# Ten first maxima of the next batch row computed beside steps 20 to 29 of the second attention, and the first maximum row turned before the overlapped stretch

## The reference

```python
# first attention: 16 heads of 8, two softmaxes of half heads, differential
a1 = softmax(q1 @ k1.T * scale); a2 = softmax(q2 @ k2.T * scale)
x = layernorm(x + rms_normed((a1 - lam * a2) @ v) @ wo)
# first network: weights and activations rounded to FP4 by blocks of 16
x = layernorm(x + fp4_linear(silu(fp4_linear(x, w_gate)) * fp4_linear(x, w_up), w_down))
# second attention: 16 query heads over 4 key heads of 64, rotary, causal
x = layernorm(x + softmax(causal(q @ k.T * scale)) @ v @ Wo + bo)
# second network: one of 8 experts for each token, relu, times the router's probability
x = layernorm(x + expert[argmax(x @ Wr)](x) * gate)
```

## Time and profile before

| | us |
|---|---|
| timed runs: lowest, median, highest | 1240.26, 1248.33, 1250.12 |
| profiled execution, its time | 1242.78 |
| profiled execution, span of its instructions | 1241.0 |
| `attention1(0)`, first to last score product (L1660) | 311.9 to 402.4 |
| `attention1(1)`, the same | 593.0 to 688.5 |
| first to last exponential of `overlap(1)` | 441.5 to 574.9 |
| first to last exponential of `overlap(2)` | 729.7 to 862.5 |

### The profile page before, as it was taken

How to read it: one execution, slowest core, us unless ns; L and a number is a source line. 1 busy time by engine, 2 the same in 40 slices (tenths; PEclk the granted TensorE clock), 3 DMA queues, 4 the chain that set the end, 5 groups by cost and what they waited for, 6 DMA issues and landing times.

```text
span 1241.0 us, 19493 instructions
## 1 busy us (share of the span) xinstructions
PE 1011.3 (81%) x6865; PEld 507.5 (41%) x6865; DVE 783.2 (63%) x1765; ACT 619.4 (50%) x1554; POOL 444.8 (36%) x545
## 2 busy tenths in 40 slices
PE   1888747889998788999988888999988829989754
PEld 1222321233454332555444442455444528344554
DVE  4898449882776688751787678770787451666421
ACT  1287514775367245774376334677177405157213
POOL 3000110301787214001776414000776450677411
PEclk7598855899999875899998875899999959999957
DMA  6300031121022001321013000320000014100051
GB/s 147 95 2 3 24 96 35 36 49 31 1 63 50 1 2 31 114 79 41 0 44 77 1 2 10 128 87 16 18 1 10 1 35 185 32 1 10 1 202 57
DMA packets 54096, 56.41 MB, mean 45 GB/s; under 512 B 13736, under 2 KB 45808, under 8 KB 53232
## 3 DMA queue, kind: packets, MB, share of 16 engines
q1 hardware_dynamic: 51968, 51.50, 14.1%
q0 software_dynamic: 1024, 2.10, 0.6%
q10 hardware_dynamic: 1008, 1.57, 0.5%
HBM read 42.77 MB, written 16.20 MB: 48 GB/s over the span
## 4 chain that ended last, share of the span: by engine, by line
PE 50%; DVE 21%; ACT 10%; issue 8%; POOL 5%; DMA 4%; SPq 1%; ACTq 0%; POOLq 0%; DVEq 0%
PE ps L1618 9%; DVE mx L987 8%; PE ps L1601 5%; PE ps L1647 5%; PE ps L1687 4%; PE ps L1660 4%; PE ps L1677 3%; ACT PROB L1317 3%; PE ps L1425 3%; PE ps L1419 2%; PE ps L1521 2%; PE ps L1436 2%; PE ps L1562 2%; DVE mx L1117 2%; ACT PROB L1275 2%
## 5 line engine op out<-in xcount | busy, mean ns | idle before, releaser
L987 DVE TENSOR_REDUCE mx<-ps 128x1 f32<-128x512 f32 x512 | 323.3, 684 | 82.1 <-PE ps L1562 79.9
L1275 ACT ACTIVATE PROB<-ps 128x512 f32<-128x512 f32 x512 | 276.8, 601 | 148.8 <-PE ps L1601 147.5
L576 POOL TENSOR_SCALAR PROB<-PROB,rsum 128x128 f32<-128x128 f32 (+3 forms) x224 | 229.6, 1036 | 76.6 <-DVE rsum L1122 76.2
L1317 ACT ACTIVATE PROB<-ps,mx 128x128 f32<-128x128 f32 (+3 forms) x256 | 133.1, 526 | 170.2 <-DVE mx L1117 169.9
L1562 PE MATMUL ps<-kst,qst 24*128 24x512 bf16 x512 | 156.4, 470 | 43.0 <-DVE mx L987 21.3
L1618 PE MATMUL ps<-PROB,v 128*32 128x256 f32 x2048 | 181.2, 446 | 3.1 <-ACT OREG L1284 2.7
L1601 PE MATMUL ps<-qst,kst 27*128 27x512 bf16 x512 | 139.8, 445 | 25.6 <-ACT PROB L1275 13.2
L1117 DVE TENSOR_REDUCE mx<-ps 128x1 f32<-128x128 f32 (+3 forms) x256 | 113.0, 484 | 69.2 <-PE ps L1662 68.9
L557 POOL CAST mparts<-mx 128x16 bf16<-128x16 f32 x32 | 7.0, 218 | 393.3 <-DVE mx L987 371.0
L1677 PE MATMUL ps<-cst,PROB 128*128 128x128 f32 x640 | 110.4, 292 | 41.9 <-ACT PROB L1332 18.2
L1660 PE MATMUL ps<-MREG,QREG 64*128 64x384 f32 (+3 forms) x512 | 108.4, 501 | 0.0
(11 more groups left out here) (220 smaller groups left out, 1361.8 us busy)
## 6 DMA issues: line engine op xcount, KB each, us to landing
wexp<-expert_rows SPq DMA_DIRECT2D x44, 514.0 KB, 5.2
qk_terms<-RREG SPq DMA_DIRECT2D x42, 128.0 KB, 2.1
qst<-qk_terms SPq DMA_DIRECT2D x16, 192.0 KB
RREG<-sorted_x SPq DMA_DIRECT2D x4, 704.0 KB, 4.7
sorted_y<-RREG SPq DMA_DIRECT2D x4, 704.0 KB, 3.9
kst<-qk_terms SPq DMA_DIRECT2D x12, 192.0 KB
expert_rows<-in_L_ffn_W_dram SPq DMA_DIRECT2D x8, 256.0 KB
expert_rows<-in_L_ffn_W_dram SPq DMA_DIRECT2D x4, 512.0 KB
```

The source lines that it names most:

```text
L576: pool.tensor_scalar(tile, tile, rsum1[:, 2 * v + half:2 * v + half + 1], None, ALU.mult).then_inc(scaled1, 1)
L987: dve.tensor_reduce(mx0[:, ga % 2, col:col + 1], ps[:, max_bank(k, MAX_SLOT[n]), :], AX, ALU.max, negate=True).then_inc(slot0_free, 1)
L1275: act.activation(prob0[:, s % 2, q % 4, q % 8 // 4], ps[:, s0_banks[q % len(s0_banks)], :], ACT.Exp, scale=float(HD0) ** -0.5).then_inc(ex ...
L1317: act.activation(prob1[:, half, at:at + w], ps[:, a1_bank(v, half), 0:w], ACT.Exp, bias=mx1[:, col:col + 1], accum_out=sum1[:, col:col + 1 ...
```

## The change

Ten maxima (n = 0 to 9) of row nx move to steps 20 to 29 of the second attention, one at the end of each step, in bank 7. The lead of steps 32 to 35 then holds the next 18 maxima (n = 10 to 27) and the first turned row, so that 28 maxima and one row precede the stretch; POOL's splitting of group 0 moves to step 33, and in the stretch the steps up to (0, 0) hold none of them. The wait for the terms stays with n = 0 and so moves to step 20; a wait for the sum of the first attention (`att0_sum`, the last reader of bank 7) joins it, and the wait for all exponentials moves to n = 10. Step 31's use of bank 7 waits until the tenth maximum is read. It concerns rows 2 and 3: `attention1(0)`, `overlap(1)`, `attention1(1)` and `overlap(2)`.

```diff
-LEAD = 18
+SINGLE, LEAD = 10, 29
+LEAD_END = (0, 0)
...
-LEAD_V = {32: ((-4, 3), (-3, 0), (-3, 1)), 33: ((-3, 2), (-3, 3)), 34: ((-2, 0), (-2, 1)), 35: ((-2, 2), (-2, 3))}
+SINGLE_V = {20 + _n: _n for _n in range(SINGLE)}
+LEAD_V = {32: ((-2, 0), (-2, 1), (-2, 2)), 33: ((-2, 3), (-1, 0)), 34: ((-1, 1), (-1, 2)), 35: ((-1, 3), (0, 0))}
...
 def max_bank(k, at):
 
+    if k >= 2 and at < SINGLE:
+        return 7
     if k >= 2 and at < LEAD:
         return 2 + at % 2
...
                 for g in range(NG):
-                    if k < BATCH:
+                    if k < BATCH and (g or k < 2):
                         max_parts0(k, g)
...
                     turn(r + 1, r + 2, v, rounds)
+                    if v == 33 and r + 2 < BATCH:
+                        max_parts0(r + 2, 0)
...
+            def maximum0(n, k):
...
+                dve.wait_ge(slot0_full, SLOTS * k + MAX_SLOT[n] + 1)
...
+                dve.tensor_reduce(mx0[:, ga % 2, col:col + 1], ps[:, max_bank(k, MAX_SLOT[n]), :], AX, ALU.max,
+                                  negate=True).then_inc(slot0_free, 1)
...
-                    if k < BATCH:
+                    if k < BATCH and (k < 2 or (s, c) > LEAD_END):
                         maxima0(s, c, k)
...
                     if nx < BATCH:
+                        if v in SINGLE_V:
+                            maximum0(SINGLE_V[v], nx)
                         for s, c in LEAD_V.get(v, ()):
                             maxima0(s, c, nx)
...
+            def score0(n, k):
...
+                if n == 0:
+                    pe.wait_ge(terms_in, 16 * 2 * HF * (k + 1))
+                    if k >= 2:
+                        pe.wait_ge(att0_sum, k)
+                if n == SINGLE and k >= 2:
+                    pe.wait_ge(exp1_done, 2 * NV * (k - 1))
+                if max_before(k, at) is not None:
+                    pe.wait_ge(slot0_free, SLOTS * k + max_before(k, at) + 1)
+                pe.matmul(ps[:, max_bank(k, at), :], qst[rows, n // 16, P * qt:P * (qt + 1)], kst[rows, n // 16, :],
+                          start=True, stop=True).then_inc(slot0_full, 1)
...
-                        scores0(s, c, k)
+                        if k < 2 or (s, c) > LEAD_END:
+                            scores0(s, c, k)
...
                         pe.wait_ge(xq_ready, k + 1)
                         pe.wait_ge(att0_sum, k + 1)
+                        if 2 <= nx < BATCH:
+                            pe.wait_ge(slot0_free, SLOTS * nx + SINGLE)
                         transpose_tiles(xq, 7, x_turned)
...
                     turn(v)
                     if nx < BATCH:
+                        if v in SINGLE_V:
+                            score0(SINGLE_V[v], nx)
                         for s, c in LEAD_V.get(v, ()):
                             scores0(s, c, nx)
```

More of the change, by code:

```diff
@@ L1549, in ffn_stream @@
                     transpose_tiles(X, 7, x_turned)
+            def score0(n, k):
+                j, qt, at = n % 4, n % 16 // 4, MAX_SLOT[n]
+                rows = slice(32 * j, 32 * j + M_ROW)
+                if n == 0:
[8 more added lines that the diff above has]
+                          start=True, stop=True).then_inc(slot0_full, 1)
             def scores0(s, c, k):
                 for n in maxima_at(s, c):
[L1554 to L1563 removed]
+                    score0(n, k)
                 for g in max_rows_at(s, c):
```

22 lines of the change are left out of this document (5 added, 17 removed).

## The result

The changed kernel takes **1257.3 us** (median of 11 runs, 1252.3 to 1260.3) where the kernel before takes 1249.5 beside it (11 runs, 1239.5 to 1251.4). The two medians lie 7.8 us apart; the ratio, worked out from all the runs, is **1.0085, 95% interval 1.0063 to 1.0107**: slower by 10.6 us (7.9 to 13.4). The forecast was 1255 us and +9.9 us. The profiled execution after spans 1255.5 us, the one before 1241.0.

What follows compares the result with a forecast made beforehand. No engine fills the 1241.0 us span; PE paces the second attention, PE and ACT lead up to (0, 1). +6.1 and +3.8 us make +9.9, added to the mean 1245.4: 1255 us, range 1244 to 1264 (8 in 10).

Steps and rivals of the forecast that it cites:

- The wait: Step 20 of both attentions: PE idle 6 and 5 us for the terms; with clock, step 24 +5.7 and +3.4 us.
- the upper bounds: Latest landing of the terms, when the input behind them lands: 383.2 and 665.9; the forecast took 381.5 and 665.3.
- The clock behind the wait: Behind step 20's wait, 4.5 us of PE work at clock 0.50, adding 2.2 us for each row, bounds 0 and 3.4.
- The products of steps 24 to 29: Steps 24 to 29 of either attention: six added products at 0.3 us, +1.5 us for each row, bounds 0.5 and 3.8.
- The turned row: Steps 32 to 35: DVE's copy and PE's turn of the row add 0.3 us for each row, bounds 0 to 0.6.
- The start of the stretch: First scores 7.0 instead of 8.5 us after the output products begin, -1.4 us for each row, bounds 1.0 and 6.5.
- the sign that I had named for this step: At the stretch's start, the first L1601 comes 7.0 us after the first L1436 if the forecast is right.
- the base: The kernel before: mean of four known executions, 1245.4 us, to which the forecast added its +9.9 us.
- The upper end of the range: 1264 us for the whole kernel: rival 2 with the terms' landing at its upper bound (+2.3).
- rival 1: At step 20 the terms land in time, at 379.2 and 662.4; +4.2 us in all, 1250 us; chance 0.25.
- rival 2: DVE bounds the second attention, each added maximum costing 0.63 us; +2.3 us for each row, 1260 us; chance 0.20.
- rival 3: DVE bounds the start of the stretch; 6.5 us won for each row instead of 1.4, 1245 us; chance 0.10.

Runs made afterwards that it cites:

- busy wait: The changed kernel with TensorE computing 24 products of constants before it waits for the terms at step 20; ratio 1.0031, +3.9 us against the kernel before.
- wait alone: The kernel before with only TensorE's wait for the next row's terms added at the end of step 20; ratio 1.0046, +5.7 us.
- with constants: The changed kernel with the ten products multiplying constants, the wait for the terms moved to step 32; ratio 1.0027, +3.4 us against the kernel before.
- with eight products: The changed kernel with eight added maxima beside steps 22 to 29 instead of ten beside 20 to 29; ratio 1.0006, +0.7 us against the kernel before.
- both short: The changed kernel with ten products of constants, these and their maxima 16 columns wide instead of 512; ratio 0.9987, -1.6 us against the kernel before.
- early queries: The changed kernel with the queries' terms loaded back before the keys' are stored; ratio 1.0045, +5.6 us against the kernel before.
- all filled: The changed kernel with queries' terms loaded early and products of constants in TensorE's idle times at four places; ratio 0.9964, -4.5 us against the kernel before.

## Why the prediction was right, and where it was not

**The wait: right.** It was predicted to hold PE behind step 20 in both attentions and to be ended by the loads of the terms, 7.2 and 6.3 us behind the start of step 20; the change shows 7.21 and 6.54 (382.69 less 375.48, 672.47 less 665.93). The choice near the upper bounds was the right one. The input behind the terms is issued at 374.73 and 663.42 after, and lands 8.5 and 9.5 us later (what answers to the earlier trace rows), so at 383.2 and 672.9: the terms land 0.5 us before it.

```profile
374.73 0.40 SPq L429 DMA_DIRECT2D XN<-in_L_attn_x_dram  x1
...
663.42 0.39 SPq L429 DMA_DIRECT2D XN<-in_L_attn_x_dram  x1
```

By the Trainium skill, "DMA: Bandwidth & Descriptors", section "Queues, rings and completion order", which the prediction cited, completion need not be in issue order. The trace does not show the order reversed: the terms, whose loads are issued from 370.98 and 660.19 on, end first, but only 0.5 us ahead of the transfer behind them, so the two ran side by side.

**The clock behind the wait: the term that was mis-sized.** 2.2 us were taken for each row. From release to step 24 the change needs 12.11 and 13.87 us where the run with the busy wait needs 8.82: 3.29 and 5.05 us. For the wait alone 2.2 was right (382.33 to 391.98 and 671.61 to 681.54, 9.65 and 9.93 for 7.68 us of work, so 2.0 and 2.3). The change's longer spells of 0.50, 10.2 and 13.7 us instead of 6.8, made the rest. So step 24 came later by 6.7 and 6.5 us, not by 5.7 and 3.4. What lengthens the spells is not settled. The added products are one candidate (with constants, of full width and without a wait for a transfer, 6.8 and 10.2 us; with narrow ones 6.8 and 6.8), but with eight products it was 6.8 and 6.8 too, and one execution of each is all that the traces have. Of the 13.2 us by which steps 20 to 24 of both rows grew, idle time makes 6.4 (11.45 less the 5.03 of step 21 before) and the clock 4.6 (8.34 less the 3.78 that the kernel before loses against 11.40, the time at the full clock); the rest, 2.2, is that of eight added products, 0.27 each.

The Trainium skill, "TensorE: Matmul & The Clock Gate", section "HAM oscillation — how this bites in real kernels", reckons the loss as half of the time at the lower clock; by that the change loses half of 10.2 and 13.7, 12.0 us, an estimate from the page. The trace agrees in direction and gives less, 3.29 + 5.05 = 8.3 us. PE still stood idle during the first 2.2 and 1.9 us of those spells, which leaves 9.9; and its work does not take twice as long at 0.50. The scores of step 21 take 1.16 us there from their start to the next row of work (673.01 to 674.17 in the change) and 0.63 at the full clock (378.37 to 379.00 in the run with the busy wait):

```profile
673.01 1.23 PE L1677 MATMUL ps<-MREG,QREG 64*128 64x256 f32 x4
674.17 0.39 PE L1679 MATMUL ps<-mask,identb 128*128 128x128 bf16 x2
...
378.37 0.70 PE L1679 MATMUL ps<-MREG,QREG 64*128 64x256 f32 x4
379.00 0.29 PE L1681 MATMUL ps<-mask,identb 128*128 128x128 bf16 x2
```

**The products of steps 24 to 29: right in size, wrong in who carries them.** 1.5 us for each row were predicted, 1.78 and 1.79 measured. The prediction let VectorE's readings lie beside PE's scores at no price and charged PE 0.3 us for each product. The readings carry two thirds or more, about 0.2 us each. VectorE is busy 9.46 of 11.17 us in steps 24 to 27, 85%, and does not become the bound that the second rival made of it. What the prediction left out is that PE waits for a reading where all maxima share one bank: 0.53 us of the 1.78.

**The turned row: 0.3 us predicted, nothing seen.** At the same clock (0.83) the run with both short takes 29.35 and 29.32 us from step 31 to the output products, as before.

**The start of the stretch: right at the full clock, which it rarely had.** Predicted were 7.0 us from the first output product to the first scores proper instead of 8.5. At the full clock it is 6.74 (four times: early queries and all filled, both rows). The change's own profile shows 9.71 and 8.29, since the clock is 0.68 and 0.80 there, the 16 first output products taking 3.78 us instead of 2.05. So the sign that I had named for this step was missing. It is not only this profile: of the 20 entries in the ten profiles with the moved maxima or constants in their place, 16 have a clock of 0.68 to 0.82 and take 8.1 to 9.7 us, and four the full clock; of the eight entries without them, two have a low clock (0.83 and 0.84, 10.0 and 9.9 us) and six the full one (8.45). In most profiles the gain of 1.7 us is lost in the clock. PE's idle time ahead of the first output product is 1.71 us with the moved maxima and 1.17 to 1.39 without (where no filling stands), but three of the four entries at the full clock have the 1.71 too, so what lowers the clock there stays open.

**The sum.** By the steps of the trace: 13.2 instead of 9.1 for steps 20 to 24, 3.6 instead of 3.0 for the products behind, about 0 instead of 0.6 for the turned row, and at an equal clock -3.4 instead of -2.8 for the entry: 13.4 against the 9.9 of the forecast and the 10.6 measured (7.9 to 13.4). Of the entry's -3.4 the profile of the change has only -0.5, for want of the clock. That the forecast met the time within 2.3 us is in part luck. The clock was taken too small, and the base, 1245.4 us, as well (the runs beside the change have a median of 1249.5); the two misses point the same way, and the timed difference came out smaller than the trace's sum, which is taken against one of the short executions of before. The upper end of the range, 1264, is 1.7 us above what its terms give (1260 and 2.3).

**The rivals.** The terms were not in time (rival 1): PE waited for them, and two steps later it did not have to, which brings most of the time back. VectorE did not become the bound (rival 2). It did not bound the entry either (rival 3): with VectorE's freed work there the entry gains 1.7 us at the full clock and not 6.5, and the next scores still wait for ACT's exponential, 0.94 us, as before (0.93).

## What to carry to other kernels

A maximum moved into an attention that TensorE fills is not free because its own wait was free elsewhere: ask what the engine's queue has to have at the new place, and when that lands; here asking two steps later nearly did. An idle time on TensorE costs twice, itself (11.5 us here, 5.0 before) and the clock behind it (8.3 us here, 3.8 before): in no run did the ten moved maxima pay for themselves, while 69 products of no use in the whole kernel, put where TensorE stands idle, gave 1.2%. Before a small gain is read from one profile, compare the granted clock of that stage in both.

## What was not expected of the hardware

Behind idle times of the same length the clock stayed at 0.50 for quite different times: 6.8 us behind 6.18 and 5.15 us of waiting without added products, 10.2 and 13.7 us behind 6.06 and 5.39 with them, and 3.4 to 10.2 us behind the 2.2 to 2.5 us of step 21, where once, in `attention1(2)` of the run with the wait alone, it did not fall at all. Twelve products of constants (2.75 us) in the place of the idle time kept it at 1.00 from step 20 to step 24 in every run that had them. And products that compute nothing made the kernel 1.2% faster, by more between step 31 and the first scores proper (8.3 us of the two rows' 12.3) than in the steps that the study had looked at.
